# Scores of two token tiles issued together in a fused attention kernel, and one last chunk of the down product a unit

## What is computed

```python
# first block, on x = layernorm(x)
q = (x @ Wq.T).reshape(b, t, 8, 64)
kv_latent = x @ Wkv_down.T
k = (kv_latent @ Wk_up.T).reshape(b, t, 8, 64)
v = (kv_latent @ Wv_up.T).reshape(b, t, 8, 64)
attn = softmax(einsum('bqhd,bkhd->bhqk', q, k) * 64 ** -0.5)
out = einsum('bhqk,bkhd->bqhd', attn, v).reshape(b, t, 512) @ Wo.T
# end of each of the 2 layers of the feed-forward stack; w2 is 682 x 256
a, g = split(h @ w1 + b1)
x = x + (a * gelu(g, approximate=False)) @ w2 + b2
```

## Time and profile before

| | us |
|---|---|
| median of 3 runs | 4440.92 |
| lowest and highest | 4433.65, 4452.77 |
| profiled execution, time | 4441.2 |
| profiled execution, span of the core | 4439.1 |

### The profile page before, as it was taken

How to read it: one execution, slowest core, us unless ns; L and a number is a source line. 1 busy time by engine, 2 the same in 40 slices (tenths; PEclk the granted TensorE clock), 3 DMA queues, 4 the chain that set the end, 5 groups by cost and what they waited for, 6 DMA issues and landing times.

```text
span 4439.1 us, 65596 instructions
## 1 busy us (share of the span) xinstructions
PE 4132.5 (93%) x23120; PEld 2596.3 (58%) x23120; DVE 3291.9 (74%) x7689; ACT 2541.6 (57%) x5480; POOL 1674.8 (38%) x1816
## 2 busy tenths in 40 slices
PE   8999989999999999987888877888999999999997
PEld 4665556666666666655555555555566666666664
DVE  5667677777767766659899999988677776677663
ACT  4555554445445445439888998876444454454441
POOL 2222355545545555430001001013565464465541
PEclk9999999999999999998889998988999999999998
DMA  2000000000001000000000001101000000100000
GB/s 79 10 16 6 24 11 6 3 3 4 24 8 30 15 8 8 26 19 20 20 21 22 22 18 28 37 18 34 3 6 3 3 25 8 32 17 17 13 20 22
DMA packets 63093, 78.57 MB, mean 18 GB/s; under 512 B 15344, under 2 KB 47392, under 8 KB 62768
## 3 DMA queue, kind: packets, MB, share of 16 engines
q1 hardware_dynamic: 62768, 74.39, 6.0%
HBM read 36.63 MB, written 12.58 MB: 11 GB/s over the span
## 4 chain that ended last, share of the span: by engine, by line
PE 65%; DVE 21%; issue 6%; ACT 5%; POOL 2%; DMA 0%; SPq 0%; POOLq 0%; DVEq 0%; ACTq 0%
PE wide L865 45%; PE o_ps L865 8%; PE wide L868 6%; PE turn_ps L868 5%; DVE x L1287 2%; DVE w_up L1387 2%; DVE turned L1338 2%; DVE prob L1399 1%; DVE w_up L1381 1%; DVE x L1393 1%; PE turn_ps L865 1%; DVE prob L1410 1%; POOL prob L1602 1%; ACT prob L1243 1%; DVE hid L1393 1%
## 5 line engine op out<-in xcount | busy, mean ns | idle before, releaser
L865 PE MATMUL wide<-x,w_up 128*128 128x512 f32 (+3 forms) x2528 | 843.0, 545 | 4.2 <-DVE x L1490 2.4
L865 PE MATMUL wide<-w_in,x_t 128*128 128x512 f32 (+2 forms) x1920 | 813.4, 568 | 17.5 <-ACT q_t L1164 8.1
L1602 POOL TENSOR_SCALAR prob<-prob,st 128x256 f32<-128x256 f32 (+1 forms) x1024 | 501.5, 508 | 758.8 <-DVE st L1423 756.4
L1223 ACT ACTIVATE prob<-prob,st 128x256 f32<-128x256 f32 (+1 forms) x1024 | 479.2, 471 | 259.9 <-DVE st L1410 259.5
L865 PEld LDWEIGHTS wide<-w_in,x_t 128*128 128x128 f32 x1920 | 342.2, 192 | 369.4 <-issue 360.6
L865 PEld LDWEIGHTS wide<-x,w_up 128*128 128x128 f32 (+2 forms) x2528 | 371.5, 195 | 289.5 <-issue 275.8
L865 PE MATMUL o_ps<-pt,v 128*32 128x128 f32 (+2 forms) x5120 | 500.0, 340 | 20.5 <-DVE pt L1439 9.9
L1575 POOL TENSOR_TENSOR sines<-raw,rot 128x512 f32<-128x512 f32 x256 | 354.0, 1403 | 331.2 <-ACT raw L1152 331.1
L1583 POOL TENSOR_TENSOR rn<-ss,minus_half 128x16 f32<-128x16 f32 x128 | 423.8, 3311 | 105.5 <-DVE ss L1333 98.7
L865 PEld LDWEIGHTS o_ps<-pt,v 128*64 128x64 f32 (+1 forms) x5120 | 322.1, 131 | 234.3 <-issue 145.6
L1254 ACT ACTIVATE o_t<-o_ps 128x512 f32<-128x512 f32 x192 | 114.2, 595 | 493.3 <-PE o_ps L865 493.3
(11 more groups left out here) (161 smaller groups left out, 7472.7 us busy)
## 6 DMA issues: line engine op xcount, KB each, us to landing
kept<-resid SPq DMA_DIRECT2D x16, 512.0 KB, 2.9
x<-kept SPq DMA_DIRECT2D x16, 512.0 KB, 3.3
w_up<-hid SPq DMA_DIRECT2D x62, 128.0 KB, 2.2
x<-hid SPq DMA_DIRECT2D x62, 128.0 KB, 2.4
shifted<-resid SPq DMA_DIRECT2D x32, 224.0 KB
w_in<-in_f_wqkv SPq DMA_DIRECT2D x4, 1536.0 KB, 6.5
w_up<-in_f_w SPq DMA_DIRECT2D x4, 1492.0 KB, 6.4
resid<-in_x SPq DMA_DIRECT2D x8, 512.0 KB, 8.9
```

Of the source, the lines that this page charges most:

```text
L865: return eng.matmul(out, lhsT, rhs, start=start, stop=stop, skip_group_check=True)
L1223: last = eng.activation(pr[:, local_span(t)], pr[:, local_span(t)], ACT.Exp, bias=sm[:, t:t + 1], scale=-1.0, accum_out=sm[:, 4 + t:5 + t])
L1602: last = eng.tensor_scalar(pr[:, local_span(t)], pr[:, local_span(t)], sm[:, 8 + t:9 + t], 1.0, ALU.mult, ALU.mult)
```

## The change

The core of the diff:

```diff
@@ cost()
     if kind in ("score", "mix") and st != "b":
-        return {"score": {"a": 1.05, "f": 1.77}, "mix": {"a": 1.85, "f": 1.65}}[kind][st] if i % 2 else 0.0
+        last = i % 4 == 3 if kind == "score" and st == "a" else i % 2
+        return {"score": {"a": 1.95, "f": 1.77}, "mix": {"a": 1.85, "f": 1.65}}[kind][st] if last else 0.0
...
     if kind == "down":
-        return 2.9 if i % 2 else 2.3
+        return 3.4 if i == TILES - 1 else 2.3
@@ parts_of()
                         put("score", i, at, final("aq_c", 1), final("ak_c"))
-                        put("low", i, at, final("score", i | 1), *freed[:1])
+                        put("low", i, at, final("score", i | 3), *freed[:1])
@@ tensor_program()
-                elif kind == "score" and i % 2 == 0:
+                elif kind == "score" and i % (4 if stage_of(u) == "a" else 2) != (3 if stage_of(u) == "a" else 1):
                     continue
...
-                    pair, t = i // 8, i // 2 % 4
-                    for j in (0, 1):
-                        r = slice(64 * j, 64 * j + 64)
-                        mm(buffers[PLACE["score", u, i - 1 + j]][:, :], q_t[s][r, pair, t * P:(t + 1) * P], k_t[s][r, 0, :],
-                           True, True).then_inc(S["score"], 1)
+                    pair = i // 8
+                    for t in (i // 2 % 4 - 1, i // 2 % 4):
+                        for j in (0, 1):
+                            r = slice(64 * j, 64 * j + 64)
+                            mm(buffers[PLACE["score", u, 8 * pair + 2 * t + j]][:, :], q_t[s][r, pair, t * P:(t + 1) * P],
+                               k_t[s][r, 0, :], True, True).then_inc(S["score"], 1)
...
-                        last = mm(ps[:, t * DIM:(t + 1) * DIM], hid[:, m, t * P:(t + 1) * P], w_down[:, m, :], m == 0, False)
-                    if i % 2:
-                        for t in DOWN_TILES[i - 1:i + 1]:
+                        last = mm(ps[:, t * DIM:(t + 1) * DIM], hid[:, m, t * P:(t + 1) * P], w_down[:, m, :], m == 0 and t % 2 == 0, False)
+                    if i == TILES - 1:
+                        for t in DOWN_TILES:
                             last = mm(ps[:, t * DIM:(t + 1) * DIM], hid[LAST_ROWS[t // 2], HC - 1, t * P:(t + 1) * P],
                                       w_down[LAST_ROWS[t // 2], HC - 1, :], False, True)
```

## The result

The changed kernel takes 4482.81 us (median of 4 runs, 4477.35 to 4485.27), the kernel before in the same comparison 4437.93 us (4433.65 to 4452.77). The ratio is 1.0088, 95% interval [1.0061, 1.0116]: slower by 0.6 to 1.2%. The forecast was 4465 us, range 4440 to 4481. Sign and mechanism came as predicted; the loss is 44 us in the traces where I had 23.5, and the median lies 2 us above the range. Set on the 4440.9 us that the forecast started from, the ratio gives 4480, the very edge of the range: the mechanism was right, and the forecast loss was about half of the measured one.

What follows compares the result with a forecast made beforehand. TensorE was taken to bound both stages. First-stage waits, less mode changes, gave +35 us and the down product -11.5, so +23.5 on 4441.2 us: 4465, range 4440 to 4481.

Steps and rivals of the forecast that it cites:

- the price of a change of mode: First-stage scores: each run has a fixed part of 0.20 us; four fewer mode changes save at most 0.8 us.
- the second four's bank: Steady first-stage unit: the second four scores wait for the third score's bank, 0.26 us.
- turn b: First stage: it shares turn a's bank and waits for ScalarE's copy, starting 1.34 us after turn a, wait 0.85.
- mix behind the last turn: First stage: the mix directly follows the fourth turn and waits for VectorE's copy of it, 0.84 us.
- The third place: Third such pattern in a first-stage unit, with aq and x transposes between its fours: about 2.1 us of waits.
- a four directly behind four turns: First stage: three fours wait for ScalarE's copy of the third turn, 0.31 us each, 0.9 in all.
- the second aq product: First stage: only two turns separate it from the first, whose copy it waits for, 0.35 us.
- Units 0 and 6: First stage: unit 0 priced as a steady unit, +5.4 us; unit 6, with next-stage work in some gaps, +4.
- The down product: Feed-forward stages: last chunk once a unit saves 0.36 us a unit, -11.5 in all, between -9 and -12.5.
- Waits as before: Rival: first-stage pressure no more than now, only the changes count, -0.8 - 11.5, 4429 us; chance 0.10.
- half of the waits: Rival: first stage adds only half of the forecast waits, +18 - 11.5, 4448 us; chance 0.28.
- More waits: Rival: first-stage turns after a mix also wait for GpSimd's scaling, +47 - 11.5, 4477 us; chance 0.14.

Runs made afterwards that it cites:

- mixwait: The changed kernel with only the order of the mix's waits altered, output bank first, then the two copies: 4488.88 us, ratio 1.0093 to the kernel before.
- quad_only: The changed kernel with the down product as before, so only the four scores issued together: 4499.1 us, ratio 1.0118 to the kernel before.
- quad_room: The changed kernel where first-stage turns, not scores, may also use banks 0 and 1: 4477.8 us, ratio 1.0073 to the kernel before.
- exp_first: The changed kernel with ScalarE's copy of the first turn behind the next four's first two exps: 4511.75 us, ratio 1.0146 to the kernel before.
- late_mix: quad_room with the first stage's mix one pair of steps later, behind the next four turns: 4436.61 us, ratio 0.9971 to the kernel before.
- four_from_2: late_mix with score pairs in units 0 and 1 and fours from unit 2: 4411.76 us, ratio 0.9914 to the kernel before.

## Why the prediction was right, and where it fell short

**What bounds the kernel, and the price of a change of mode.** Right. A run of four takes 1.92 us (1.91 predicted), and the edit of the scores brought nothing but waits.

**The waits of a steady unit.** The mechanism held link by link. Forecast and measured, for each "four, mix, four, turns, mix": the second four's bank 0.26, 0.32; turn b 0.85, 0.85; third turn 0.23, 0.23; fourth turn 0.18, 0.23; mix behind the last turn 0.84, 1.11. Together 2.36, 2.74. The third place 2.1, 2.42; a four directly behind four turns 0.31, 0.41; the second aq product 0.35, 0.50. The unit's waits are 9.8 us for 8.1 forecast. The term that was too small is the last link, and mixwait shows part of why: I let TensorE follow 0.05 us after a copy, as behind a single wait, but the mix and the fours have several waits, and 0.11 us of the excess is the order of these. (With some 0.2 us in other places these make the 9.8.) From +5.4 to +6.7 in the five steady units (1 to 5): 6 us of the miss.

**Units 0 and 6.** Here the step failed. I gave unit 0 the price of a steady unit and unit 6 a discount to +4, because work of the next stage would stand in the gaps. From last mix to last mix unit 6 takes 82.4 us for 69.2, +13.2: its waits are 11.5 us for 1.5. The unit had few waits before, and the fours made the chain in it too. One of its waits is no link of the chain: GpSimd, which has the next stage's work between its scalings, is at that stage's `rn` for 2.90 us, the scaling that a turn needs comes behind it, and TensorE waits 2.55 us. Its clock is then 0.51 for 3.40 us, in which it makes the 16 turns that take some 1.8 us at 1.00. POOL, PE and a window of PE alone (length, busy, clock, DMA share, GB/s) in after:

```profile
542.18 2.90 POOL L1585 TENSOR_TENSOR rn<-ss,minus_half 128x16 f32<-128x16 f32 x1 [1.34 <-DVE ss L1335]
545.07 2.30 POOL L1607 TENSOR_SCALAR prob<-prob,st 128x512 f32<-128x512 f32 x2
```

```profile
545.86 1.06 PE L869 MATMUL turn_ps<-ident,prob 128*128 128x128 f32 x4 [2.55 <-POOL prob L1607]
```

```profile
545.86:549.26 3.40, 3.40 (x16) 0.51 0.00 0
```

So the next stage's work, which I had filling gaps, stood in the way on GpSimd, and that makes about 4 of the 13.2 us. quad_only and mixwait have the same wait of 2.55 us, and in before TensorE waits for GpSimd nowhere between 75 and 600 us. No run takes this wait away by itself.

Unit 0 takes 119.1 for 106.6, +12.5, more than a steady one. There the clock shares in it; a window of the start, before and then after:

```profile
45.00:60.00 15.00, 14.79 (x76) 8.96 (x76) 12.74 (x32) 10.72 (x25) 4.34 (x5) 1.00 0.00 1
```

```profile
45.00:60.00 15.00, 11.98 (x54) 6.48 (x53) 9.77 (x26) 6.56 (x13) 2.82 (x3) 0.93 0.00 1
```

TensorE idles 3 us of 15, 1.90 of it in one wait for an exp ahead of the second four, and is granted 0.93 in the mean. (About 2.4 us of unit 0 are a longer first aq product, which other runs have or don't have without regard to the edits; in quad_only and mixwait, which don't have it, unit 0 takes 117.2 and 114.8 us, so that the edit's own part is 8 to 11 us.) Unit 7 came out at -1.5 (0, between -5 and +5, forecast), and units 8 to 10 gave back 4.7 us, which I had not counted; I take it that the next stage's chain was further on, which no run tells apart. In sum +53 at the last mix of unit 10 where +35 was forecast: 6 more from the size of the links, 7 from unit 0, 9 from unit 6, and 6 less from units 7 to 10; the rest is rounding and the 0.8 us that the forecast took off for changes of mode.

**The down product.** Right in size: -0.34 to -0.36 a steady unit, 24 such units. From unit 10's last mix to the end after is 9.0 us faster than before, with 1.7 lost in units 32 and 33 on the way. For -11.5 forecast I should have left out the units at the borders, which wait for other things. The lower bound, -9, was there. The 9.0 itself is in part luck: it holds stage b, which took 1148.7 and 1148.8 us in these two executions and 1144 to 1163 in those of the other kernels. The steady units carry the reading.

**The rivals.** "Waits as before" and "half of the waits" are refuted: the steady unit has the whole chain. "More waits" (4477) named nearly the right size for a reason that holds in one place only: GpSimd's scaling ends none of the waits of after's steady units, and the one of 2.55 us in unit 6. The case I left out was a loss in the units that are not steady; the range should have reached over it. The rule of the Trainium skill in "TensorEngine Tiling (Array Packing)" that row tiling adds to PSUM pressure is borne out in sign, but quad_room shows that the pressure alone is 0.3 to 1.0 of 6.7 us a unit.

## What to carry to other kernels

Joining small jobs on the bounding engine saves their fixed part only where they were apart, and it makes their results arrive in bursts: look at what stood between a producer and the consumer of its copy, since those pieces were the cover. When a chain of copies loses its cover, more buffers move the wait and don't remove it; let the consumer run one group later (and then give it the buffers). Price the units at a pipeline's start and end by themselves: here units 0 and 6 lost 8 to 13 us where a steady unit lost 6.7, and work of the next stage can stand ahead of this one's on a helper engine instead of filling a gap.

## What the runs showed of the hardware

- TensorE's clock fell to 0.50 in a stretch of 6 us in which it was busy for 2.70, and its mix then took 3.61 us for 1.88 (exp_first); in unit 6 of after it was at 0.51 for 3.40 us behind a wait of 2.55 us; the shorter waits of after, 0.85 to 1.1 us at a time, leave it at 1.00 in the steady units. It cost 2.4 us on top of the wait in exp_first and about 1.6 in unit 6 of after. The Trainium skill, "TensorE: Matmul & The Clock Gate", Part 1, tells of a gate that halves the clock when the engine has been little busy; this trace agrees.
- Several waits ahead of one matmul are worked off one behind another: in after the records of TensorE's waits ahead of the mix stand at 319.90 and 320.01 us and the mix at 320.12, and with the blocking one last the matmul starts 0.11 us sooner (mixwait: 0.15 us after the copy's end for 0.26).
- Stage b (units 24 to 31), which no edit touches, took 1144 to 1163 us in the profiled executions; the granted clock from 1960 to 3040 us was 0.84 in late_mix (1163 us) and 0.87 in four_from_2 (1144 us), and DVE and ACT, which carry that stage, did less in the same time (late_mix, then four_from_2; PE, PEld, DVE, ACT, POOL, clock):

```profile
1960.00:3040.00 1080.00, 904.69 (x6686) 575.70 (x6686) 991.15 (x2013) 918.05 (x1618) 107.22 (x128) 0.84 0.08 22
```

```profile
1960.00:3040.00 1080.00, 885.16 (x6802) 565.32 (x6800) 1010.63 (x2075) 937.58 (x1662) 108.86 (x133) 0.87 0.08 22
```

  In one execution of each kernel that is as large as the differences that were to be judged; the sums by stage, not the spans, told the experiments apart. What sets it was not studied.
